# Two relative-position attention layers on one core: group-wise order, new PSUM bank plan, split store

## What is computed

```python
q, k, v = proj_heads(wq, bq), proj_heads(wk, bk), proj_heads(wv, bv)
attn = einsum('bqd,bkd->bqk', q * scale, k)
rel_h = einsum('bhwc,hkc->bhwk', rq, Rh)
rel_w = einsum('bhwc,wkc->bhwk', rq, Rw)
attn = attn + rel_h[..., :, None] + rel_w[..., None, :]
out = softmax(attn) @ v
x = x + out @ wo + bo            # and the same again with the second layer's weights
```

## Time and profile before

| | us |
|---|---|
| runs | 80.12, 82.45, 82.57 |
| median | 82.45 |
| profiled execution | 79.96 |
| its span, first to last instruction | 78.0 |

### The profile page before, as it was taken

One profiled execution on the slowest core, in us unless ns is written; L12 is line 12 of the kernel. 1 busy time (PEld: TensorE's weight loads), 2 busy tenths in 40 slices (PEclk: granted clock), 3 DMA queues, 4 the chain that ended last, 5 costly groups with the idle time before them and its releaser, 6 DMA issues.

```text
span 78.0 us, 1573 instructions
## 1 busy us (share of the span) xinstructions
PE 68.4 (88%) x603; PEld 55.1 (71%) x603; DVE 45.0 (58%) x102; ACT 51.8 (66%) x98; POOL 14.5 (19%) x49
## 2 busy tenths in 40 slices
PE   4995989999869999979999899999978999978850
PEld 4994869998656985824767789998666984924730
DVE  3945997686945685322256579677846675422210
ACT  5439997999979787661330094999979787571310
POOL 5874992000111111000003000000121121000000
PEclk9999999999999999999999999999999999999997
DMA  0968100000000000000000000000000000000003
GB/s 10 302 146 255 35 0 8 0 0 0 0 0 4 4 0 8 0 0 0 0 0 0 8 0 0 0 0 0 0 0 0 8 0 0 0 0 0 8 0 101
DMA packets 1543, 1.75 MB, mean 22 GB/s; under 512 B 312, under 2 KB 1146, under 8 KB 1536
## 3 DMA queue, kind: packets, MB, share of 16 engines
q1 hardware_dynamic: 1536, 1.66, 7.1%
HBM read 1.46 MB, written 0.20 MB: 21 GB/s over the span
## 4 chain that ended last, share of the span: by engine, by line
PE 74%; DVE 13%; ACT 4%; issue 4%; POOL 1%; DVEq 0%; ACTq 0%
PE ps L738 10%; PE ps L638 8%; PE ps L584 8%; PE ps L510 7%; PE ps L598 7%; PE ps L620 7%; PE ps L569 4%; PE ps L718 4%; ACT qs L276 3%; PE ps L648 3%; PE ps L610 3%; PE ps L697 3%; DVE table L468 2%; PE ps L541 2%; PE ps L555 2%
## 5 line engine op out<-in xcount | busy, mean ns | idle before, releaser
L407 DVE TENSOR_REDUCE nm<-ps 128x2 f32<-128x512 f32 x24 | 15.5, 686 | 7.3 <-PE ps L584 7.2
L324 ACT ACTIVATE pt<-ps 128x1024 f32<-128x1024 f32 x12 | 12.3, 1024 | 1.5 <-PE ps L620 0.5
L276 ACT ACTIVATE qs<-ps 64x512 fp32r<-64x512 f32 x20 | 11.8, 589 | 0.4
L584 PE MATMUL ps<-ks,qs 128*128 128x256 f32 x48 | 8.8, 300 | 0.5 <-DVE nm L407 0.3
L510 PE MATMUL ps<-busy 128*128 128x128 bf16 x87 | 8.0, 256 | 1.5 <-DVE busy L373 1.1
L262 POOL CAST nmhl<-nm 128x4 fp32r<-128x4 f32 x12 | 2.2, 187 | 36.1 <-DVE nm L407 36.1
L738 PEld LDWEIGHTS ps<-zq,table 128*64 128x64 f32 x128 | 7.9, 138 | 0.8 <-issue 0.6
L510 PEld LDWEIGHTS ps<-busy 128*128 128x128 bf16 x87 | 6.8, 119 | 2.2 <-DVE busy L373 1.1
L738 PE MATMUL ps<-zq,table 128*64 128x48 f32 x128 | 8.0, 216 | 0.3 <-DVE zq L478 0.3
L620 PE MATMUL ps<-nmt,ones 128*128 128x512 f32 x24 | 8.2, 420 | 0.1
L598 PE MATMUL ps<-qs,ks 128*128 128x256 f32 x48 | 8.2, 293 | 0.0
(11 more groups left out here) (94 smaller groups left out, 105.8 us busy)
## 6 DMA issues: line engine op xcount, KB each, us to landing
win<-in_w_in_dram SPq DMA_DIRECT2D x4, 216.0 KB
xt<-in_x_dram SPq DMA_DIRECT2D x1, 192.0 KB, 2.3
wout<-in_w_out_dram SPq DMA_DIRECT2D x2, 96.0 KB
out_dram<-res SPq DMA_DIRECT2D x1, 192.0 KB, 2.0
wout<-in_w_out_dram SPq DMA_DIRECT2D x2, 48.0 KB
rel_raw<-in_rel_dram SPq DMA_DIRECT2D x1, 62.0 KB, 2.7
win<-in_w_in_dram SPq DMA_DIRECT2D x2, 2.2 KB
wout<-in_w_out_dram SPq DMA_DIRECT2D x2, 0.8 KB
```

What stands on the lines that cost most here:

```text
L276: return act.activation(dst, src, ACT.Copy, scale=scale)
L324: act.activation(pt[:, p, :, :, :].rearrange("p a k t -> p a (k t)"), ps[:, ST_BANK[p % 2]:ST_BANK[p % 2] + 2, :], ACT.Exp, scale=SCALE[l] ...
L407: dve.tensor_reduce(nm[:, p, a, :], ps[:, S_BANK[a], :].rearrange("p (t k) -> p t k", k=T), AX.X, ALU.max, negate=True).then_inc(max_sb, 1)
L584: last = mm(ps[:, S_BANK[a], t * T:(t + 1) * T], qs[:, 2 * p + a, t * P:(t + 1) * P], ks[:, 2 * p + a, :], start=True, stop=True)
```

## The change

- The order on PE goes by groups of heads. The q and k chunks of bank 0 are completed first. `query_rows(0)` stands before the tables, `key_rows(0)` inside their first loop, the two `values` after the tables. The first scores need the moves of group 0 alone. Group 1's relative rows and group 2's key rows stand behind the first scores, group 2's query and relative rows around the maxima of the first pairs.
- A new bank plan. All relative rows use bank 2 one after the other, q and k rows share banks 0, 1 and 3, scores use 4 and 5, transposed scores 6, 7, 0, 1. Both tiles of v lie in one bank, and DVE copies them with one instruction.
- The moves are split 12 on ACT and 6 on DVE.
- The dummy products between the maxima are removed; those at the start and around the group norm stay.
- Two of the four one-hot copies go from ACT to POOL.
- The result is stored in two halves, one issued by ACT, one by SP.

```diff
-        X_BANK = [3, 4]
-        GN_BANK = 6
-        V_BANK = [3, 0]
+        X_BANK = [6, 7]
+        GN_BANK = 4
+        V_BANK = 3
         REL_BANK = 4
-        K_BANK, Q_BANK, R_BANK = [0, 1, 2], [3, 5, 2], [4, 6, 7]
-        S_BANK = [0, 1]
-        ST_BANK = [3, 5]
-        O_BANK, NM_BANK = [2, 2, 1], 7
-        ONT_BANK = [7, 2]
-        Y_BANK = 3
-        LORA_BANK = [0, 7]
-        ACT_MOVES = [("k", 0, 0), ("k", 1, 0), ("k", 1, 1), ("k", 2, 0), ("k", 2, 1),
-                     ("q", 0, 0), ("r", 0, 0), ("q", 1, 0), ("q", 1, 1), ("r", 1, 0), ("r", 1, 1),
-                     ("r", 2, 0), ("r", 2, 1), ("q", 2, 0), ("q", 2, 1)]
-        DVE_MOVES = [("k", 0, 1), ("q", 0, 1), ("r", 0, 1)]
-        BUSY_WITH_MAXIMA = [8, 5]
+        K_BANK, Q_BANK, R_BANK = [1, 0, 3], [0, 1, 2], [2, 2, 2]
+        S_BANK = [4, 5]
+        ST_BANK = [6, 0]
+        O_BANK, NM_BANK = [2, 2, 5], 3
+        ONT_BANK = [3, 2]
+        Y_BANK = 6
+        LORA_BANK = [2, 3]
+        ACT_MOVES = [("q", 0, 0), ("k", 0, 0), ("k", 1, 0), ("q", 1, 0), ("r", 0, 0), ("q", 1, 1),
+                     ("k", 2, 0), ("k", 2, 1), ("r", 1, 0), ("r", 1, 1), ("q", 2, 0), ("r", 2, 0)]
+        DVE_MOVES = [("q", 0, 1), ("k", 0, 1), ("k", 1, 1), ("r", 0, 1), ("q", 2, 1), ("r", 2, 1)]
...
-            sp.wait_ge(res_act, 1)
             sp.wait_ge(res_dve, 1)
-            sp.dma_start(out_tokens, res[:, :, :]).then_inc(stored, 16)
-            sp.wait_ge(stored, 16)
+            sp.dma_start(out_tokens[:, 1, :], res[:, 1, :]).then_inc(stored, 16)
+            sp.wait_ge(stored, 32)
...
+            for n in range(2, 4):
+                pool.tensor_copy(key_onehots(n), onehots).then_inc(made_keys, 1)
+            pool.wait_ge(made_keys, 4)
...
-                    for n in range(3):
-                        key_onehots(n)
+                    for n in range(2):
+                        act.wait_ge(zeroed, 9)
+                        copy(key_onehots(n), onehots).then_inc(made_keys, 1)
...
-                    if l == 0 and which == 1:
-                        key_onehots(3)
+                move(l, 0)
                 for which in range(2):
                     for half in range(2):
                         act.wait_ge(rel_ps, 4 * l + 2 * which + half + 1)
                         copy(rel_dst(rr_hi, which, half), rel_src(which, half)).then_inc(rr_hi_sb, 1)
-                    if which == 0:
-                        for n in range(3):
-                            move(l, n)
-                for n in range(3, 13):
+                        if which == 0 and half == 0:
+                            move(l, 1)
+                for n in range(2, 10):
                     move(l, n)
                 max_rows(l, 0)
-                for n in range(13, 15):
-                    move(l, n)
-                for p in range(PAIRS):
+                move(l, 10)
+                probabilities(l, 0)
+                max_rows(l, 1)
+                move(l, 11)
+                max_rows(l, 2)
+                for p in range(1, PAIRS):
                     probabilities(l, p)
-                    if p == 0:
-                        max_rows(l, 1)
                     if p + 2 < PAIRS:
                         max_rows(l, p + 2)
...
             copy(res[:, 0, :], ps[:, Y_BANK, 0:C]).then_inc(res_act, 1)
+            act.wait_ge(res_act, 1)
+            act.dma_start(out_tokens[:, 0, :], res[:, 0, :]).then_inc(stored, 16)
...
-                values(l, 0)
+                move(l, 0)
                 for which in range(2):
                     for half in range(2):
...
-                    if which == 0:
-                        move(l, 0)
-                move(l, 1)
-                values(l, 1)
+                        if which == 0 and half == 0:
+                            move(l, 1)
                 move(l, 2)
-                for p in range(PAIRS):
+                move(l, 3)
+                values(l)
+                maxima(l, 0)
+                maxima(l, 1)
+                move(l, 4)
+                maxima(l, 2)
+                move(l, 5)
+                for p in range(3, PAIRS):
                     maxima(l, p)
...
             def key_rows(l, g):
                 if g == 0:
                     pe.wait_ge(made_pick, 2)
-                    pe.wait_ge(z_lo, 6 * l + 6)
+                    pe.wait_ge(z_lo, 6 * l + NG + 1)
+                elif g == 1:
+                    pe.wait_ge(z_lo, 6 * l + NG + 2)
+                    moved(l, *both("q", 0))
+                else:
+                    pe.wait_ge(z_lo, 6 * l + NG + 3)
+                    pe.wait_ge(v_sb, l + 1)
...
             def query_rows(l, g):
                 if g == 0:
                     pe.wait_ge(made_pick, 6)
-                    pe.wait_ge(v_sb, TT * l + 1)
+                    pe.wait_ge(z_lo, 6 * l + 2)
                 elif g == 1:
-                    pe.wait_ge(rr_lo_sb, 4 * l + 4)
+                    moved(l, *both("k", 0))
                 else:
-                    moved(l, *both("k", 2))
+                    moved(l, *both("r", 1))
...
             def relative_rows(l, g):
-                pe.wait_ge(pick_zero, 2)
-                if g > 0:
-                    pe.wait_ge(rr_lo_sb, 4 * l + 4)
+                if g == 0:
+                    pe.wait_ge(pick_zero, 2)
+                    pe.wait_ge(z_lo, 6 * l + 6)
+                elif g == 1:
+                    moved(l, *both("r", 0))
                 else:
-                    pe.wait_ge(rr_lo_sb, 4 * l + 1)
+                    moved(l, *both("q", 2))
...
             def scores(l, p, heads=(0, 1)):
-                if p == 0 and 0 in heads:
+                if p == 0:
                     pe.wait_ge(made_keys, 4)
-                    moved(l, *(m for g in range(NG) for m in both("k", g)))
-                    pe.wait_ge(v_sb, TT * l + 2)
-                moved(l, *both("q", p // 2), *both("r", p // 2))
+                    pe.wait_ge(rr_lo_sb, 4 * l + 4)
+                moved(l, *both("k", p // 2), *both("q", p // 2), *both("r", p // 2))
...
             def turn_max(l, p):
                 if p == 0:
                     pe.wait_ge(made_ident_r, 1)
-                    moved(l, *both("r", 2))
+                    moved(l, *both("k", 2))
...
-                for ic, m in ((0, 0), (0, 1), (1, 0), (1, 1), (0, 2), (1, 2)):
+                for ic, m in ((0, 0), (1, 0), (0, 1), (1, 1), (0, 2), (1, 2)):
...
-                if l == 1:
-                    pe.wait_ge(wl_sb, 2)
-                values(l, 0)
-
+                query_rows(l, 0)
                 if l == 0:
                     pe.wait_ge(tab_sb, 4)
...
-                    if which == 0:
-                        key_rows(l, 0)
-                        key_rows(l, 1)
+                        if which == 0 and i == 7:
+                            key_rows(l, 0)
+
+                key_rows(l, 1)
+                query_rows(l, 1)
+                if l == 1:
+                    pe.wait_ge(wl_sb, 2)
+                values(l, 0)
+                relative_rows(l, 0)
+                values(l, 1)
+                scores(l, 0)
+                relative_rows(l, 1)
                 key_rows(l, 2)
-
-                query_rows(l, 0)
-                values(l, 1)
-                relative_rows(l, 0)
-                query_rows(l, 1)
-                relative_rows(l, 1)
-                relative_rows(l, 2)
-                query_rows(l, 2)
-                scores(l, 0)
                 scores_t(l, 0)
                 scores(l, 1)
                 scores_t(l, 1)
                 turn_max(l, 0)
-                scores(l, 2)
+                query_rows(l, 2)
+                scores(l, 2, (0,))
                 add_max(l, 0)
+                scores(l, 2, (1,))
                 turn_max(l, 1)
-                moved(l, *both("q", 2))
-                keep_busy(BUSY_WITH_MAXIMA[0], bank=O_BANK[0])
+                relative_rows(l, 2)
                 for p in range(PAIRS):
...
-                    if p == 0:
-                        keep_busy(BUSY_WITH_MAXIMA[1], bank=O_BANK[0])
```

More of the change, by code:

```diff
@@ L201, in move_args, with key_onehots @@
                     done, NG * l + g + 1)
+        def key_onehots(n):
+            return ks[64:P, 3 * n:3 * n + 3, :]
+        onehots = onehot[64:P, :, :].rearrange("p a b -> p (a b)").unsqueeze(1).to_broadcast([64, 3, T])
         @block.gpsimd
@@ L250, in _ @@
             pool.memset(nmt[:, :, :].bitcast(F32), 0.0).then_inc(nmt_zero, 1)
+            pool.wait_ge(made_ones4, 1)
+            pool.wait_ge(nmt_zero, 1)
+            for n in range(2, 4):
+                pool.tensor_copy(key_onehots(n), onehots).then_inc(made_keys, 1)
+            pool.wait_ge(made_keys, 4)
             pool.memset(lora_rows[:, :, :], 0.0).then_inc(lora_zero, 1)
@@ L302, in _ @@
             copy(pick_rl[:, :, 32:64], by_pos).then_inc(made_pick, 1)
[L304 to L308, removed]
             def move(l, n):
@@ L412, in out_columns, with values @@
```

(26 more changed lines are left out.)

## The result

Over 20 executions of each kernel the changed one has a median of 80.48 us (78.66 to 83.48), the one before 80.12 (79.71 to 83.55). Between the executions of both kernels whose granted clock stayed up, the ratio is **0.9855, 95% interval 0.9831 to 0.9879**: 1.2 us less. The other seven have a median of 78.74. The median of before is 80.12 over these 20 executions; the 82.45 that the prediction started from came from its first three.

The account below looks back on a forecast made before the run. Preparation was taken as bound by ACT and PE's order, the rest by PE's work. Layer 1 0.8, layer 0 0.6 and store 0.15 gave 1.55 us; off the 82.45 median, 80.9 us, range 77.9 to 82.0.

Parts of the forecast that it names:

- the base: Median 82.45 us of three timed runs before, from which the 1.55 us was taken to give 80.9.
- The rival on the clock: PE's clock falls in the maxima: about +5 us per layer at worst, +2 if half hit in one layer; chance 0.08.
- Steps 1 to 3: Layer 1, QKV products to first scores: tables 0.27 earlier, scores at 53.05 against 54.29, first maximum 1.23 earlier.
- Step 4: Layer 1, before third query rows: PE idles 1.1 us behind ACT's row of four moves; `add_max(0)` 1.1 earlier.
- Step 5: Layer 1, DVE's row of moves and maxima, pairs 2 and 3: `add_max(1)` 0.9 earlier, `add_max(2)` only 0.53.
- Step 6: Layer 1, after `add_max(2)`: PE runs through, `add_max(3)` at 63.8 against 64.60; 0.8 us won in the layer.
- Layer 0: z waits for DVE's tables, so step 1 (QKV order) gives 0.05 to 0.1; the rest as layer 1; 0.6 us won.
- POOL's one-hot copies: Two copies moved to POOL, 0.8 to 2 us each, ending by 15 us before scores need them: no cost.
- Store: Kernel end, result stored in two halves: 0.15 us won, from nothing or a 0.2 loss up to 0.4.

Follow-up runs that it names:

- fill_gap: Changed kernel plus eight dummy products in layer 0 between the QKV products and the first query rows; ratio to before 0.9857 [0.9831, 0.9883].
- swap_fill: swap plus eight dummy products in layer 0 between the QKV products and the first query rows; ratio to before 0.977 [0.9711, 0.9829].
- swap: Changed kernel with r1 moved before k2 and third query rows before the turn of the first maxima; ratio to before 0.9711, 77.7 us at full clock.
- b_nodummy: Kernel before without its eight and five dummy products between the maxima; ratio 1.0000 [0.9981, 1.0018].
- b_split: Kernel before with its store split in two halves from ACT's and SP's queue, nothing else; ratio 0.9939 [0.9919, 0.9960].

## Why the prediction was right and wrong

The number was 80.9 with 1.55 us won. The gain was 1.2 to 1.4 at full clock, and the median 80.48 lies in the range; yet against the median before of 80.12 it did not go down at all. Two steps failed, and that they nearly cancel in the number is luck.

**The first step that failed is the base.** The prediction wrote that "the profiled one lies at their fast end. Taken off the median, 82.45 gives 80.9". It took the spread of 80.12 to 82.57 as a scatter that both kernels share, around a middle at 82.45. The runs show two levels of the kernel before: about 80.1 at full granted clock, and 81.8 to 84.0 at a mean of 0.94 to 0.96. The right base for a sum made from a trace at clock 0.993 was that trace's level, and 79.96 less 1.55 is 78.4, against 78.7 measured there. The prediction had this number and left it. The base was 2.3 too high.

**The second is that the clock's loss stood at nothing in the sum.** The rival on the clock had the effect (slower, +2 or more in one layer) but put it in the maxima, where the dummies had gone and PE rests, and gave it 0.08. In no trace did the grant fall there. It fell in or right behind the tables, mostly while PE was busy, and in over half of the executions. It lifted the changed kernel's median from 78.74 at full clock to 80.48, by 1.7, and that is why the median did not go down. What could have warned was the spread itself: by their times two of the three runs of before were already down. The next question would have been which stretch of the change loses dense products, and that is the surroundings of the tables. The Trainium skill (TensorE: Matmul & The Clock Gate, A second HAM failure mode), which the prediction weighed, ties the swing to short rests between groups of products. The traces here neither show nor exclude that: seven of eight falls lie where PE had been busy for 2 us or more, though a rest of 0.53 stood ahead of the four in layer 0, and one fall lies 0.6 behind a rest of 0.34. Eight dummies in that rest of layer 0 left 1 of 5 (fill_gap) and 3 of 6 (swap_fill) lowered.

Step by step, at full clock:

- Steps 1 to 3, layer 1. Tables 0.43 earlier, not 0.27: PE starts the query rows 2.60 behind the first product, sooner than the products' modelled end of 2.86. First scores 1.28 earlier, foretold 1.24. The values copy took 0.56, as taken.
- Step 4. The rest before the third query rows is 0.91 (foretold 1.1) and ACT's row the one named; swap shows it to be worth 1.0 in two layers, so it was rightly called the place where the gain is given back.
- Step 5. The DVE row was right in its order. `add_max(1)` won 0.76, foretold 0.9, and `add_max(2)` 0.35, foretold 0.53. The claim that most of the 0.9 would be lost without the removal of the dummies was too strong: with dummies of half width back in the changed order, `add_max(1)` is 0.42 later. In the kernel before they cost nothing (b_nodummy is at 1.0000), covered by ACT, whose copy of the second maxima stands behind its first exponential.
- Step 6. `add_max(3)` 0.65 earlier, foretold 0.8.
- Layer 0. Foretold 0.6, found 0.27. This term was mis-sized: the stage from tables to `add_max(3)` wins only 0.22 to 0.28 in either layer, and the 0.43 that layer 1 wins ahead of it is missing here, as z waits for DVE's tables. The walk had split layer 1 as 0.27 and 0.53.
- POOL's one-hot copies: the two took 1.60 together, inside 0.8 to 2 each, and nothing waited for them.
- Store. Foretold 0.15 with an upper bound of 0.4. In the old order b_split measures 0.5 (0.3 to 0.65): the landing itself shortens, which the prediction left out. In the changed kernel the longer last wait takes most of it back, and about 0.1 is left, so 0.15 is near for a reason that the prediction did not have. The rule of the Trainium skill that was weighed there (DMA: Bandwidth & Descriptors, Issuing engines are not separate DMA queues) gives no more than the issue time, 0.37; b_split's middle of 0.5 lies above that, though its interval reaches down to 0.3, and the landing, 1.7 in place of 2.0, is shorter beyond the rule.

The terms seen in the traces of the changed order are 0.65 + 0.27 + 0.1, some 1.0, and the span of fill_gap is 1.0 under that of the kernel before (77.0 and 78.0). The runs at full clock differ by 1.2 to 1.4; the 0.2 to 0.4 between them no trace shows. The chances gave 0.46 to within 2%, which is where the ratio lies.

Open: what about the tables lowers the clock. DVE is also busier beside the tables now (in layer 1 for 3.98 of 4.20 us from 48.80, before for 3.39 of 4.50 from 46.50), and that was not tried alone. With dummies ahead of or inside them in layer 0, 6 of 17 executions were down, with the values alone put back 7 of 18; only values and key rows together came near the old share, with 2 of 12, and each count is small. No kernel of the old order was traced with a lowered clock, so where it falls there is not shown. It wasn't tried to take the values out of the kernel before alone.

## What to carry to other kernels

Before a sum is taken off a median, look whether the runs fall into levels and take the level of the trace. Filler on the chain of waits is free when the next real instruction waits for another engine: look for who is late once it is gone. In a hand-written order, ask of every wait what stands behind it on its engine; here one edge (which of two pairs of moves ACT makes first, with PE's order to match) was worth 1.0 us, almost as much as the whole change. And read a gain where it ends: most of the store's 0.5 was gone again at the last wait of the changed kernel.

## What was new about the hardware

The granted clock fell to 0.50 in the middle of a stretch in which PE was busy without a rest (10.70 to 20 us in the changed kernel), in tables of 48 columns on 64 columns of weights, and came back 3 to 7 us later. Rests of 0.9 elsewhere stood at a grant of 1.00. A fall cost 1.2 and 3.0 us between tables and first scores in the two traces of the changed kernel (8.12 and 9.86 against 6.90). And storing 192 KB as two halves from two queues was worth 0.5 us in the kernel before (0.3 to 0.65), with the landing 1.7 us behind the issue in place of 2.0; one issue takes 0.37.
